# A recommendation head on one Trainium2 core: the bias pass as three matmuls of 32 rows

## The reference

```
all_embed = jnp.concatenate([users_emb_w[users], items_emb_w[items]], axis=1)
h = jax.nn.relu(all_embed @ w1.T + b1)
h = jax.nn.relu(h @ w2.T + b2)
cross = jax.nn.one_hot(items, NUM_ITEMS, dtype=h.dtype)
head_in = jnp.concatenate([cross, h], axis=1)
return jax.nn.sigmoid(head_in @ w_head.T + b_head)
```

## Time and profile before

| | |
|---|---|
| median of three executions | 69.0 us (68.83 to 69.25) |
| the profiled execution | 68.38 us |
| its span, first to last instruction | 66.5 us |
| granted TensorE clock | 0.998 of full |
| PE busy | 57.2 us (86%) |
| VectorE busy | 42.1 us (63%) |
| ScalarE busy | 38.5 us (58%) |
| GpSimd busy | 31.3 us (47%) |
| moved by DMA | 21.86 MB, mean 329 GB/s |

### The profile page before, as it was taken

One profiled execution on the slowest core, in us unless ns is written; L12 is line 12 of the kernel. 1 busy time (PEld: TensorE's weight loads), 2 busy tenths in 40 slices (PEclk: granted clock), 3 DMA queues, 4 the chain that ended last, 5 costly groups with the idle time before them and its releaser, 6 DMA issues.

```text
span 66.5 us, 864 instructions
## 1 busy us (share of the span) xinstructions
PE 57.2 (86%) x284; PEld 42.7 (64%) x284; DVE 42.1 (63%) x93; ACT 38.5 (58%) x71; POOL 31.3 (47%) x38
## 2 busy tenths in 40 slices
PE   1999976999999997959999999999999998998000
PEld 1344355776888885838886888787877867876000
DVE  3811167558869684936795969586868676579200
ACT  0713904336667659372586666849494857589600
POOL 4287787687687688688686755550000000000000
PEclk9999999999999999999999999999999999999999
DMA  0489998898999899899999999999999996717992
GB/s 0 53 322 342 279 334 271 192 346 265 210 371 357 294 395 402 261 406 419 417 421 409 421 422 417 414 421 417 425 416 407 410 417 243 319 72 313 383 374 85
DMA packets 6496, 21.86 MB, mean 329 GB/s; under 512 B 1372, under 2 KB 2012, under 8 KB 6492
## 3 DMA queue, kind: packets, MB, share of 16 engines
q0 software_dynamic: 2816, 10.77, 46.4%
q1 hardware_dynamic: 3100, 10.29, 38.8%
q10 hardware_dynamic: 576, 0.76, 3.8%
HBM read 11.56 MB, written 10.24 MB: 328 GB/s over the span
## 4 chain that ended last, share of the span: by engine, by line
DMA 33%; POOL 33%; issue 13%; PE 6%; ACT 4%; DVE 2%; POOLq 2%
DMA rows<-user_rows,idx 30%; POOL rows L167 17%; POOL rows L171 16%; PE acc L318 4%; DMA idx<-pairs 3%; ACT rows L288 2%; ACT rows L292 2%; POOLq L43 2%; DVE rows L240 1%; PE ps_h L314 0%; PE ps_x L301 0%; DVE emb L208 0%; DVE emb L206 0%; PE ps_h L310 0%; PE ps_h L309 0%
## 5 line engine op out<-in xcount | busy, mean ns | idle before, releaser
L221 DVE TENSOR_TENSOR rows<-acc,rows 128x1250 f32<-128x1250 f32 x14 | 20.4, 1459 | 1.1
L167 POOL DMA_INDIRECT rows<-item_rows,idx x16 | 15.4, 964 | 7.4 <-issue 3.7
L275 ACT ACTIVATE rows<-rows 128x1250 f32<-128x1250 f32 x14 | 17.5, 1248 | 0.0
L171 POOL DMA_INDIRECT rows<-user_rows,idx x16 | 15.1, 947 | 4.9 <-issue 4.9
L318 PE MATMUL acc<-w_hid_lo,h2T_hi 128*128 128x512 f32 (+1 forms) x45 | 12.3, 381 | 0.0
L318 PE MATMUL acc<-w_hid_hi,h2T_lo 128*128 128x512 f32 (+1 forms) x45 | 12.2, 379 | 0.0
L318 PE MATMUL acc<-w_hid_hi,h2T_hi 128*128 128x512 f32 (+1 forms) x45 | 11.8, 369 | 0.0
L262 ACT ACTIVATE h1T<-ps_h,b_sb 128x128 f32<-128x128 f32 x16 | 5.9, 367 | 9.9 <-PE ps_h L310 9.9
L318 PE MATMUL acc<-bias_parts,bias_sel 128*128 128x512 f32 (+1 forms) x45 | 11.3, 359 | 0.0
L266 ACT ACTIVATE h2T_hi<-ps_h,b_sb 128x128 fp32r<-128x128 f32 x16 | 5.9, 368 | 9.3 <-PE ps_h L314 9.3
L212 DVE CAST embT<-ps_x 128x128 fp32r<-128x128 f32 x16 | 4.7, 293 | 7.5 <-PE ps_x L301 7.5
(11 more groups left out here) (39 smaller groups left out, 50.3 us busy)
## 6 DMA issues: line engine op xcount, KB each, us to landing
probs<-rows SPq DMA_DIRECT2D x14, 625.0 KB, 7.2
w_hid_f<-w_hiddenT ACTq DMA_DIRECT2D x1, 625.0 KB
probs<-rows SPq DMA_DIRECT2D x2, 312.5 KB, 3.0
probs<-rows SPq DMA_DIRECT2D x2, 256.0 KB, 3.4
rows<-item_rows,idx POOLq DMA_INDIRECT x16, 7.4
rows<-user_rows,idx POOLq DMA_INDIRECT x16, 7.8
probs<-rows ACTq DMA_DIRECT2D x1, 113.0 KB, 3.5
w1T_f<-w1T SPq DMA_DIRECT2D x2, 32.0 KB
```

What stands on the lines that cost most here:

```text
L167: nc.gpsimd.indirect_dma_start(out=rows[:, at + UD:at + ROW], out_offset=None, in_=item_rows, in_offset=bass.IndirectOffsetOnAxis(ap=idx[: ...
L171: nc.gpsimd.indirect_dma_start(out=rows[:, at:at + UD], out_offset=None, in_=user_rows, in_offset=bass.IndirectOffsetOnAxis(ap=idx[:, 2 * ...
L221: nc.vector.tensor_tensor(logits(t), acc[t % SLOTS][:, 0:N], logits(t), ALU.add).then_inc(s_sum, 1)
L275: nc.scalar.activation(logits(t), logits(t), ACT.Sigmoid).then_inc(s_prob, 1)
```

## The change

The bias pass becomes three matmuls of 32 rows each. The ones of `bias_sel` stand in rows 0 and 1, 32 and 33, 64 and 65, and so do the bias's high and low part in `bias_parts`. The matmul of bank 0 reads rows 0 to 31 of both, that of bank 1 rows 32 to 63, that of bank 2 rows 64 to 95. So each uses another group of 32 rows of PE's array; the columns and the results are as before. To fill the rows there are three memsets of ones instead of one, and six row copies instead of two: the high parts on SP's queue, the low parts on ScalarE's, ahead of the two copies of `w_hid_f`. In the last tile the bias pass now comes whole, before all three banks, and before the waits for h2.

```diff
+GROUP = 32
@@ sync @@
-            for r, part in enumerate((bias_hi, bias_lo)):
-                sp.dma_start(bias_parts[r:r + 1, :].bitcast(F32).rearrange("a (p c) -> a p c", p=BP),
-                             part[:].bitcast(F32)).then_inc(s_bias_row, 16)
+            for g in range(BANKS):
+                sp.dma_start(bias_parts[g * GROUP:g * GROUP + 1, :].bitcast(F32).rearrange("a (p c) -> a p c", p=BP),
+                             bias_hi[:].bitcast(F32)).then_inc(s_bias_row, 16)
@@ vector @@
-            nc.vector.memset(bias_sel[0:2, :].bitcast(F32), 1.0).then_inc(s_const, 1)
+            for g in range(BANKS):
+                nc.vector.memset(bias_sel[g * GROUP:g * GROUP + 2, :].bitcast(F32), 1.0).then_inc(s_const, 1)
@@ scalar @@
             nc.scalar.activation(warm[:], warm[:], ACT.Sigmoid)
+            act.wait_ge(s_const, 3)
+            act.wait_ge(s_bias_split, 2)
+            for g in range(BANKS):
+                at = g * GROUP + 1
+                act.dma_start(bias_parts[at:at + 1, :].bitcast(F32).rearrange("a (p c) -> a p c", p=BP),
+                              bias_lo[:].bitcast(F32)).then_inc(s_bias_row, 16)
             act.wait_ge(s_hidden, 16)
@@ bias_pass @@
-                one_pass(t, bias_sel[:], bias_parts, True, False)
+                for g, (c, n) in enumerate(chunks):
+                    at = g * GROUP
+                    nc.tensor.matmul(acc[t % SLOTS][:, c:c + n], bias_sel[at:at + GROUP, :],
+                                     bias_parts[at:at + GROUP, c:c + n], start=True, stop=False)
@@ last_head @@
-                pe.wait_ge(s_sum, t - SLOTS + 1)
+                bias_pass(t)
                 pe.wait_ge(s_h2_hi, t + 1)
                 pe.wait_ge(s_h2_lo, t + 1)
-                terms = [(bias_sel[:], bias_parts), (hi, w_hid_hi), (hi, w_hid_lo), (lo, w_hid_hi)]
+                terms = [(hi, w_hid_hi), (hi, w_hid_lo), (lo, w_hid_hi)]
@@ tensor @@
-            pe.wait_ge(s_const, 4)
-            pe.wait_ge(s_bias_row, 32)
+            pe.wait_ge(s_const, 3 + BANKS)
+            pe.wait_ge(s_bias_row, 32 * BANKS)
```

More of the change, by code:

```diff
@@ L350, in last_head @@
                         last = nc.tensor.matmul(acc[s][:, c:c + n], h, w[:, c:c + n],
-                                                start=(k == 0), stop=(k == len(terms) - 1))
+                                                start=False, stop=(k == len(terms) - 1))
                     last.then_inc(s_last_acc, 1)
```

## The result

The changed kernel took 70.07 us (69.9 to 70.52, four executions), the kernel before 69.09 us (68.83 to 69.25) beside it: ratio 1.016, interval 1.011 to 1.021. It is slower by about 1.0 us; no change was forecast, and the range ended at 69.7. The span of the profiled execution grew from 66.5 to 68.3 us. In five of the eight groups of runs behind the experiments the kernel before itself took 97 to 98 us, and in their profiles engines stood still for up to 25 us waiting for events: the times of those runs are given, but of their traces only the undisturbed stretches are used.

A forecast was written before the change was run, and what follows sets the result against it. DMA transfers at 400 to 425 GB/s were taken to set the pace, PE bounding a minority of cycles. Span 66.5 - 0.19 (tail) + 0 (middle) + 0 (start) = 66.3; on the median 68.8 us, range 68.3 to 69.7.

The forecast's parts named there:

- the start: First microseconds: six row copies instead of two, last SP row landing at 8.9 us, no delay, 0 in the sum.
- what a late start costs: Start to end: 1.1 us of delay leaves 0.17 MB unmoved by the DMA engines, costing 0.4 us.
- the price of a change of size: Each bias pass: going to 32 rows and coming back each cost one cold start, 0.08 us; pass 0.39 us.
- the -0.19 of the tail: Tail: tile 14's bias pass lies wholly on the path, so its shortening moves everything after it by 0.19 us.
- full emptying: Bias pass: both size changes wait for results to leave the array, adding 0.34 us; pass 0.73 us, 0.15 us lost.
- the other side: Bias pass: the view that the change of size empties the array, the same as rival 2; chance 0.22.
- rival 2: Every bias pass: size change empties the array, pass 0.73 us or more, 69.2 to 69.4 us, up to 76; chance 0.22.
- rival 4: Bias passes: no overlap, no cost, matmuls take turns as before at 0.58 us, time 69.0 us; chance 0.14.
- The sign that I had named: On PE, first bias matmul to L309 (layer 1): 0.39 us by the forecast, 0.23, 0.58 or 0.7 and more otherwise.
- The middle: Cycles between start and tail: shorter passes gain up to 0.8 us, lost again waiting for rows; counted as 0.
- the bank order of the last tile: Tile 15: whole bias pass ahead of all banks, bank 0 complete at 60.06 us, before VectorE is free at 60.40; hidden.
- the full overlap: Bias pass: all three matmuls together, 0.23 us, 0.35 us off the tail, time 68.3 to 68.65 us; chance 0.20.

The follow-up runs named there:

- start-only kernel: Kernel before with only the changed start (three small memsets, six row copies, PE waiting for all six), 128-row passes: 69.86 us against 69.11, ratio 1.007.
- start-warm kernel: The start-only kernel with two more warming matmuls before the wait for the bias rows: 70.18 us against 69.04, too scattered for an interval.
- pass only: Changed kernel, six copies on SP, PE waiting only for rows 0 and 1, passes 0 and 1 using that one group: 69.89 us against 69.11, ratio 1.011.
- changed, warm: Changed kernel with two more warming matmuls before the wait for the bias rows: 69.83 us against 68.9, ratio 1.009.
- later passes: Kernel before, its start and passes 0 and 1 kept, passes 2 to 15 as 32-row passes in three groups: 69.34 us against 68.9, ratio 1.003.

## Why the prediction was wrong

Three steps of the prediction failed: the start, put at 0 in the sum; what a late start costs, 0.4 us for 1.1; and the price of a change of size, taken as 0.08 us, from which the -0.19 of the tail came.

**The start, the step that cost the time.** I had SP's last copy issued at 5.6 us and took the middle of its landing, 8.9 us, "and no delay". VectorE's three memsets took 0.65 us and both queues began at 4.28 instead of 3.8. I reckoned ScalarE's queue only for what stood behind it, not for the landing of its own last row: its first issue took 1.57 us, the third began at 6.65, and PE was released by that row at 10.94. The landing, 4.3 us, was within my 1.9 to 4.6; the issue time and the choice of the middle were wrong. At the longest landing I had, behind this issue, it would have been 11.2 us. In the start-only kernel the same row took 5.3 us, more than any landing that I had looked at.

**What lateness costs, also failed.** I had 0.4 us for 1.1 us of delay. The first addition was 3.0 us late, since PE at half clock added 1.1: from the first bias pass to the first addition 6.67 us, against 5.56 in the kernel before and 5.58 in the start-warm kernel. The term for bytes not moved was right in kind; the wider hole at the end I didn't have. With 3.0 us instead of 1.1 my rate gives 1.1 us; the span grew by 1.8, the medians lie 1.0 apart. I had also misread: the engines do not move 400 to 425 GB/s from 18 us on, but 261 to 402 until 28 us (351 from 18 to 30), and only then run full. The late outputs fall in just that stretch.

**The clock was in no rival.** In the rows it fell after an idle 1.4 to 1.5 us in the first tiles (changed, start only), and also without that idle when passes 0 and 1 had 32 rows (pass only, longest idle 0.61 us; changed, warm, 0.98 us), and did not in two profiles with 128-row passes and no such idle (later passes, 0.61 us; start, warm, 0.96 us). Two pairs of profiles point at the 32-row passes. But the fall doesn't come every time. A span of 68 us with 3.4 us at half clock has a mean clock of at most 0.975 (an estimate from these two numbers). In the changed kernel with more warming matmuls four of ten executions had 0.989 to 0.999, so no such fall; they took 69.1, 69.5, 69.5 and 70.5 us. In the start-only kernel two of ten had 0.983 and 0.985 and took 69.0 us both, no more than the kernel before, while the other eight, at 0.934 to 0.975, took 69.5 to 70.7. All four executions of the changed kernel lie at 0.938 to 0.972. Whether the rows also landed earlier in the two quick ones no trace shows. So the clock is part of the loss, partly by chance, and what brings its fall is not settled.

**The pass, also failed: a term of the wrong size.** The mechanism was right: the overlap is real, and a change of size is not free. I took 0.08 us for each change, from the cold start; it is 0.18 or so (0.37 for the pair). That is near the 0.17 of "full emptying", which I had put on top of the 0.08 for the other side. With the overlap it makes 0.23 + 0.37 = 0.60, the 0.58 of before. So the mechanism of rival 2 was there, with the result of rival 4: a saving of 0.19 us was forecast, -0.04 came. The sign that I had named, from the first bias matmul to layer 1, came out at 0.43, near my 0.39, and would have misled me: about half of the price falls outside it, 0.08 us ahead of the pass and 0.10 between the two matmuls of layer 1.

**Right.** The middle was counted as nothing, and nothing came, but not for my reason (that VectorE would wait at the next landing): the pass saved nothing there. That PE, once late, bounds the cycles for long (additions 2.99 us apart from 20 to 44 us) was not in the prediction. Right with its reason: the bank order of the last tile hidden (tile 15's first addition starts 1.44 us after tile 14's, 60.78 to 62.22, as before); w_hid's copies hidden, if barely: the first 1.35 us late, the second ending at 9.77, VectorE reading at 9.88 instead of 9.52.

One slip among the chances: I gave 0.22 to a gain of over 0.35 us, more than the 0.20 of the full overlap on which it rested.

**What makes up the 1.6%.** Start alone 0.7% (0.2 to 1.3), later passes alone 0.3% (-0.2 to 0.8), passes 0 and 1 with 32 rows, by pass-only less later passes, some 0.8%, in which two passes in one group stand that the changed kernel doesn't have. Added up they meet the whole, each with an uncertainty nearly as large as the part; that the parts add up is not shown. What is shown is where the loss is: with the start and passes 0 and 1 as before it can't be told from none.

## What to carry to other kernels

Matmuls of 32 rows in different groups overlap fully, but going to them and back cost 0.37 us here: a group of them between 128-row work has to save more than that, and three of 512, 512 and 226 columns save 0.33. Look at what an edit adds to the first microseconds: here a row that landed 1.9 us late ahead of everything on PE, with half clock behind it, stood at the head of a loss of 1.0 us, where the DMA engines are full from 28 us on. For each copy on which a start waits, follow its queue to its last issue and add at least the longest landing seen, not the middle.

## What was not expected of the hardware

The granted clock fell to half for 3.4 us in the first tiles, after idle stretches of 1.4 to 1.5 us or, where 32-row passes stood, with no more idle than the kernel before has (0.61 us, pass only) or 0.98 us (changed, warm). In the changed kernel the way from the first bias pass to the first addition was 1.1 us longer. ScalarE's first row copy took 1.57 us to issue when SP's, 0.83 us, began at the same time, 4.28 us. The next ones, begun 0.06 us apart (5.89 and 5.94), took 0.73 and 0.72, so that the other queue is busy does not by itself make an issue long.
